# Where the sum over a head group's samples and a batch's routing slots stand in a step-by-step schedule

## The reference

```python
sk = 0.5 * (w0 * _gather_pad0(Kh, i0) + w1 * _gather_pad0(Kh, i1))
sv = 0.5 * (w0 * _gather_pad0(Vh, i0) + w1 * _gather_pad0(Vh, i1))
scores = jnp.einsum('bhqd,bhqkd->bhqk', Qh / math.sqrt(HD), sk)
attn = jax.nn.softmax(scores, axis=-1)
ctx = jnp.einsum('bhqk,bhqkd->bhqd', attn, sv)
...
scores = jax.nn.sigmoid(router_logits.astype(jnp.float32))
_, topk_ids = jax.lax.top_k(scores + e_bias[None, :], K)
```

## Time and profile before

| | us |
|---|---|
| median of 3 runs | 995.78 (994.69 to 996.07) |
| span of the profiled execution, first to last instruction | 992.6 |
| busy: PE / DVE / ACT / POOL | 639.3 / 623.1 / 423.5 / 379.0 |
| POOL, indirect DMAs of L585 | 78.5 (64 of them) |
| POOL, products of L580 | 44.4 (16 of them) |

### The profile page before, as it was taken

One profiled execution on the slowest core, in us unless ns is written; L12 is line 12 of the kernel. 1 busy time (PEld: TensorE's weight loads), 2 busy tenths in 40 slices (PEclk: granted clock), 3 DMA queues, 4 the chain that ended last, 5 costly groups with the idle time before them and its releaser, 6 DMA issues.

```text
span 992.6 us, 14085 instructions
## 1 busy us (share of the span) xinstructions
PE 639.3 (64%) x3898; PEld 398.8 (40%) x3927; DVE 623.1 (63%) x1579; ACT 423.5 (43%) x906; POOL 379.0 (38%) x345
## 2 busy tenths in 40 slices
PE   4487887776658361778781636777763221899991
PEld 2243343243224240577650313343432111787881
DVE  2678998878948887257533633877755667343443
ACT  2484866676758231344440213443542000343442
POOL 2314223554361388000016887183420000665641
PEclk9997996897979666699995677988996555899996
DMA  5795875564545022244423311000002000111115
GB/s 148 231 309 178 291 255 176 170 205 154 181 175 174 9 83 79 78 125 122 117 79 112 137 42 38 1 16 1 12 10 97 0 0 1 44 41 40 44 32 138
DMA packets 82754, 102.84 MB, mean 104 GB/s; under 512 B 11317, under 2 KB 66169, under 8 KB 82298
## 3 DMA queue, kind: packets, MB, share of 16 engines
q1 hardware_dynamic: 58618, 80.04, 25.1%
q0 software_dynamic: 6592, 13.51, 4.5%
q10 hardware_dynamic: 17472, 8.39, 2.9%
HBM read 82.25 MB, written 19.66 MB: 103 GB/s over the span
## 4 chain that ended last, share of the span: by engine, by line
PE 35%; DVE 32%; ACT 8%; issue 7%; POOL 6%; DMA 6%; another core or an unknown queue 4%; SPq 2%; ACTq 0%; DVEq 0%; POOLq 0%
POOL xs L585 4%; DVE oh L1176 4%; PE PS L1981 4%; DMA oh<-index 4%; DVE nmx L1313 3%; PE PS L1959 3%; PE PS L1964 3%; PE PS L1789 2%; PE PS L1890 2%; PE PS L1972 2%; PE PS L1781 2%; DVE pkr L1140 2%; DVE pk L1189 1%; DVE ctok L1167 1%
## 5 line engine op out<-in xcount | busy, mean ns | idle before, releaser
L617 POOL DMA_INDIRECT yb<-ys,yrow x64 | 61.5, 960 | 139.8 <-DMA ys<-y 117.8
L1176 DVE TENSOR_SCALAR oh<-oh,pcol 128x2048 bf16<-128x2048 bf16 x80 | 75.1, 939 | 26.6 <-DMA oh<-index 25.6
L585 POOL DMA_INDIRECT xs<-xn,row x64 | 78.5, 1226 | 32.3 <-issue 18.6
L1692 PE MATMUL PS<-oh,T 128*128 128x512 bf16 x211 | 67.4, 425 | 27.2 <-ACT oh L778 24.4
L580 POOL TENSOR_TENSOR vv<-vv,coef 128x1280 f32<-128x1280 f32 x16 | 44.4, 2772 | 98.1 <-DVE coef L1160 89.1
L683 POOL DMA_INDIRECT xg<-xrows,tok x39 | 37.5, 962 | 107.6 <-DVE tok L1522 96.0
L1697 PE MATMUL PS<-oh,T 128*32 128x512 bf16 x960 | 76.2, 422 | 1.9 <-issue 1.8
L1706 PE MATMUL PS<-ident,gs 128*128 128x128 f32 x320 | 56.8, 304 | 23.5 <-ACT vv L799 22.8
L1313 DVE TENSOR_REDUCE nmx<-PS 128x4 f32<-128x616 f32 x64 | 48.8, 793 | 27.5 <-remote 18.5
L777 ACT ACTIVATE oh<-oh,pcol 128x512 bf16<-128x512 bf16 x80 | 57.7, 721 | 15.5 <-DMA oh<-index 15.5
L1706 PEld LDWEIGHTS PS<-ident,gs 128*128 128x128 f32 x320 | 36.6, 151 | 62.0 <-issue 48.3
(11 more groups left out here) (370 smaller groups left out, 1729.6 us busy)
## 6 DMA issues: line engine op xcount, KB each, us to landing
oh<-index SPq DMA_DIRECT2D x80, 512.0 KB
oh<-index SPq DMA_DIRECT2D x80, 128.0 KB
x<-xs SPq DMA_DIRECT2D x96, 64.0 KB, 1.9
ys<-y ACTq DMA_DIRECT2D x48, 128.0 KB, 2.2
w0r<-in_w SPq DMA_DIRECT2D x8, 384.0 KB, 5.8
xs<-nil SPq DMA_DIRECT2D x8, 256.0 KB
wg1r<-in_wg SPq DMA_DIRECT2D x1, 2048.0 KB
wu1r<-in_wu SPq DMA_DIRECT2D x1, 2048.0 KB
```

What stands on the lines that cost most here:

```text
L585: pool.indirect_dma_start(xs[:], bass.IndirectOffsetOnAxis(ap=row0[:, QT * b + t, k:k + 1], axis=0), xn1[:, b % 2, t, :], None).then_inc(s ...
L617: pool.indirect_dma_start(yb[:, b % 2, t, k, :], None, ys[:], bass.IndirectOffsetOnAxis(ap=yrow0[:, QT * b + t, k:k + 1], axis=0))\
L1176: dve.tensor_scalar(main, main, pcol[:, 0:1], None, ALU.is_equal).then_inc(s["oh_main"], 1)
L1692: pe.matmul(o, T2[:, b % 2, p, n // NK, :], oh[:, slot, GH, :], start=(p == 0), stop=False, skip_group_check=True)
```

## The change

The product of POOL moves from step 5q + 11 to step 5q + 9, and the sum on DVE from step 5q + 13 to step 5q + 10, for all groups alike (the two extra cases for the last group fall away: its product stands at step 84 and its sum at step 85). Since weights stand at step 5q + 8, the sum follows them by two steps and not by five. All parts of `post` stand three steps earlier. No instruction is added or removed.

```diff
-POST_SLOTS = {9: [9], 10: [10], 11: [11], 12: [13], 13: [14], 14: [15], 15: [16], 16: [17], 17: [19], 18: [20], 19: [21, 22],
-              20: [23], 21: [24], 22: [25], 23: [26], 24: [27]}
+POST_SLOTS = {6: [9], 7: [10], 8: [11], 9: [13], 10: [14], 11: [15], 12: [16], 13: [17], 14: [19], 15: [20], 16: [21, 22],
+              17: [23], 18: [24], 19: [25], 20: [26], 21: [27]}
@@ gpsimd
-                if (g - 6) % NK == 0 and g >= 11 and g < ALL_STEPS + 6:
-                    weigh_values((g - 6) // NK - 1)
-                if g == ALL_STEPS + 1:
-                    weigh_values(B * NG - 1)
+                if g % NK == NK - 1 and NK < g < ALL_STEPS + NK:
+                    weigh_values(g // NK - 1)
@@ vector
-                if k == 1 and 2 <= q <= B * NG:
-                    combine(q - 2)
-                if m == ALL_STEPS + 2:
-                    combine(B * NG - 1)
+                if k == 3 and 1 <= q <= B * NG:
+                    combine(q - 1)
```

## The result

The changed kernel takes 1007.7 us (median of 4 runs, 1005.9 to 1011.2) against 995.8 (four runs too, 994.7 to 996.1): a ratio of 1.0133, with a 95% interval of 1.0085 to 1.0182. It is slower by 11.9 us. A second profile of each kernel, on another chip, gave a ratio of 1.0120 (1.0047 to 1.0194). The first profiled execution of the changed kernel spans 1009.4 us, 16.8 more than that of before; 11.4 of it are in the first stage, the rest fell in later stages and did not come again (second pair of profiles: 998.4 and 1010.5, and from the start of the expert stage to the end 595.2 and 595.7). So the place of the stage's end, the first L1261 (before: L1265) on DVE, is the surest measure here: 401.97 before, 413.38 after; in the second pair 403.2 and 414.8.

The account below looks back on a forecast made before the run. The first stage's end was taken to be bound by POOL's scatters, and before them by DVE's chain. +16.8 (last product behind scatters) - 2.5 (batch 3's empty queue) + 0 (loop) = +14.3: 1010 us, range 1000 to 1019.

Parts of the forecast that it names:

- Part (a): On POOL, the last group's product now stands behind batch 2's 16 scatters; the last sum starts 16.8 us later.
- T: Time when DVE ends step 77, which makes batch 2's row numbers; forecast 332.4 us.
- carry-in from the earlier batches: Delay that batches 0 and 1 bring into the time of batch 2's row numbers; forecast +2 us.
- the idle time that the added work fills: Part of DVE's 6.7 us of added work by step 77 absorbed in waits; taken as 2 us, bounds zero and about 7.
- Part (b): The same exchange of products and scatters for batches 0 and 1; +1 us each, bounds -3 and +6 for batch 0.
- Part (c): Batch 3's scatters meet an empty POOL queue and start at their row numbers; -2.5 us, bounds 0 and 4.5.
- Part (d): Sum and product nearer in the loop: late sums and one-hot collisions against earlier norm parts easing PE's waits; set at 0.
- The sum: Total of all terms: +14.3 us on the span of 992.6, giving 1006.9, or 1010 measured.
- Faster: Rival: scatters hide if T to the last weights exceeds 24 us, and earlier rows win; 982 to 993 us, 8%.
- The small case: Rival: POOL's queue is short and only the loop's one-hot collisions cost 2 to 5 us; 998 to 1001 us, 5%.
- the larger one: Rival: stands at steps 45 and 65 are uncovered because PE stops too, 5 us each more; 1018 to 1024 us, 13%.
- The signs named: Last product behind 16 scatters, DVE's last sum idle 8 us or more, sums at steps 40 and 80 standing 2 to 5.

Follow-up runs that it names:

- Kernel 3: The changed kernel, but POOL issues batch 2's 16 scatters behind the last product; ratio 1.0006 to the kernel before, 992.4 against 993.9 us.
- kernel 1: The kernel before with only DVE's sum moved (step 5q + 13 to 5q + 10); ratio 1.0114, 1006.2 against 993.9 us.
- kernel 7: The kernel before with product and sum moved, routing slots unmoved, batches 0 and 1 scattering in two halves, batch 2 behind the last product; ratio 1.0051.
- kernel 8: The kernel before, only with batches 0 and 1 scattering in two halves with a product between; ratio 0.9917, 948.6 against 956.2 us.
- kernel 6: The changed kernel with at most 8 scatters between products for batches 0 and 1, and 8 of batch 2's 16 ahead of the last product; ratio 0.9940.
- kernel 5: The changed kernel with at most 8 scatters between products for batches 0 and 1, and 4 of batch 2's 16 ahead of the last product; ratio 0.9909.
- kernel 2: The kernel before with product and sum moved but not the routing slots; ratio 1.0106 to the kernel before, 1006.6 us.

## Why the prediction was right

- **Part (a), the step that decides, held in mechanism, place and size.** Row numbers of batch 2 (T) were forecast at 332.4 and came at 330.35; the first scatter to the end of the last product was forecast at 26.5 us and took 25.4 (330.63 to 356.00). The last sum began at 356.04, forecast 358.9: +14.0 and not +16.8. The scatters took 1.27 each, the fast price, where 1.32 was taken. The weights of the last group were forecast near T + 14.5 and came at T + 13.9, so POOL ended last by 9.0 us, as forecast. Kernel 3, with these 16 scatters behind the last product, has its last sum at 342.09: net of all the rest, nothing else is in the 14.0 us.
- **T** was forecast 2.0 us too late. The carry-in from the earlier batches was as forecast: the `pk` of steps 66 and 67, where batch 2's parts begin, come 2.0 us later than before. The term that was mis-sized is the idle time that the added work fills: of the 6.7 us only 2.65 show (330.35 - 325.7 - 2.0), so 4.05 were absorbed and not 2. The bounds (0 and 7) held it. Both figures come from one profile of each kernel.
- **Part (b), the stands for batches 0 and 1**, forecast at +1 and +1. The sum of step 45 was forecast at 206 after 8 us of standing, and began at 207.51 after 6.3. But the `pk` of step 49 is 4.4 us later than before, not 1, and from there to step 66 the changed kernel gains 2.4 us, because the kernel before stands itself at steps 64 to 66. The stand that was forecast alike for step 65 is 0.4 us. So each term was mis-sized, within the bounds of -3 and +6, and their sum, 2.0, was right by luck. It is luck of the place, too: in kernel 1 the same kind of stand, twice as long, was carried to the end with 13 us, where I had expected 3 to 8.
- **Part (c)**: forecast -2.5. From the last sum to the stage's end it takes 57.3 us after (356.04 to 413.38) and 59.9 before (342.07 to 401.97): -2.6. The first two scatters of batch 3 (1.80 and 1.87 us) are slowed as the last two of batch 2 were in the same place before (1.82 and 1.84).
- **Part (d), set at nothing, was right at most as a net sum, and its two sides stay open.** At step 81 kernel 7 is 10.6 us behind kernel 8, which hasn't the moved pair, and 6.4 behind kernel 6, which has the earlier slots as well. But 10.3 us of stands for POOL are in kernel 7, so neither figure is the price of one side of (d) alone. In the changed kernel both sides are mixed with the stand that the kernel before has at steps 64 to 66, where the changed one loses 7 us less (7.3 against 14.5).
- **The sum**: +14.0 (a, b) - 2.6 (c) = +11.4 in the first stage, and the medians moved by 11.9; forecast +14.3. The difference is T (2.0) and the scatters and products (1.1), less 0.3 from the row numbers to the first scatter.
- **The rivals.** Faster needed 24 us from T to the last weights; it took 13.9 (330.35 to 344.27). The small case and the larger one did not come in the changed kernel. The signs named all came (the two sums at steps 40 and 80 stood 4.5 and 4.0 us), but the last product began at 353.29 (forecast near 356) and the stage's last scatter ended at 406.86 (forecast near 410).

The Trainium skill's page SBUF — State Buffer, section "SBUF: two separate sides", says that GpSimd cannot write the descriptors of its DMAs while DVE is in an operation in two-port mode. The trace agrees as far as it goes: the twelve scatters at 338.34 to 353.27 took 1.27 from start to start, while DVE had sums and small operations up to 344.27 and nothing after. The slow ones of the tail, 2.2 us from start to start, stand beside DVE's L1238, a TENSOR_TENSOR of f32 with two inputs; that kind of operation the page's box on such DMAs does not name, so the 2.2 us are what this trace shows, and the prediction's 1.91 beside the same operation is no proof of the box.

## What to carry to other kernels

An engine's list is a queue: before two things are moved nearer to each other, look at what else stands between them on every engine that they pass, and ask whether a batch's long burst (here 16 issues of 1.27 us) now stands ahead of a short step that the tail hangs on. A burst that nobody waits for belongs behind the short step, or in pieces between such steps: kernel 8 is 0.8% faster than the kernel before with this alone, and kernel 5, which is the changed kernel with its scatters placed so, 0.9%. A stand in the middle of a loop is only covered where the kernel stood before; it is not to be counted as free elsewhere.

## What was not expected of the hardware

The stand at steps 64 to 66 came in both profiles of the kernel before, on different chips, 14.5 and 12.9 us from the `pk` of step 64 to that of step 66, in the middle of a burst of 16 scatters. It takes 2.0 us where the burst came later and 2.8 to 6.8 where it came in halves (8.6 in kernel 7, 4.8 of them DVE's wait for POOL's product). It takes 7.3 in the changed kernel, whose burst was near its end (286.0) when PE came there. Kernels 1 and 2 take 18.6 and 13.6 us, of which 13.1 and 8.8 are DVE's wait for POOL; in kernel 2 ACT's copy of sample 64 was not late although the burst was as old (that of sample 65 came 3.1 us behind it). The profile names issue or an unknown releaser. In the two profiles of the kernel before, PE's record has samples 64 and 65 done 7 to 13 us before the copies that wait for them begin; whether PE, ACT or the signal between them is late, and whether loading a part of a program has to do with it, was not tried, and stays open.
